# Reordered head of an attention and mixture-of-experts kernel: two router buffers, first-half tiles among the last own ones, two attention tiles ahead of expert 0, tiles spread evenly over the experts

## What is computed

```python
xn = _layernorm(x, axis=-1)
# attention: k = exp(10i * (xn @ Wk)), v = xn @ Wv, 16 heads of 64
out_pos   = real(cumsum(v * rotors) * conj(rotors)) / sqrt(t + 1)
out_assoc = real(cumsum(v * conj(roll(k, 1))) * k) / sqrt(t + 1)
attn = (0.5 * out_pos + 0.5 * out_assoc) @ Wo
# experts: every token goes to one of 8 experts, the argmax of its router logits
p = softmax(xn @ gate_w); e = argmax(p)
ffn = p[e] * (gelu(xn @ w1[e]) @ w2[e])      # 1024 -> 4096 -> 1024
x = x + attn + ffn
```

## Time and profile before

| | |
|---|---|
| median of 3 runs | 1130.99 us (1130.82 to 1131.71) |
| the profiled execution | 1131.58 us; its slowest core, core 1, spans 1129.5 us from the first instruction to the last |
| spans of the eight cores | 1120.4 to 1129.5 us |
| first matmul of expert 0 / 3 / 6 / 7 on core 1 | 131.9 / 474.5 / 819.1 / 926.4 us |
| busy share: TensorE, VectorE, ScalarE, GpSimd | 83%, 61%, 53%, 14% |

### The profile page before, as it was taken

How to read it: one execution, slowest core, us unless ns; L and a number is a source line. 1 busy time by engine, 2 the same in 40 slices (tenths; PEclk the granted TensorE clock), 3 DMA queues, 4 the chain that set the end, 5 groups by cost and what they waited for, 6 DMA issues and landing times.

```text
span 1129.5 us, 18153 instructions; the slowest of 8 cores (1120.4 to 1129.5 us)
## 1 busy us (share of the span) xinstructions
PE 935.5 (83%) x6296; PEld 609.3 (54%) x6296; DVE 692.5 (61%) x1498; ACT 597.7 (53%) x1014; POOL 161.6 (14%) x184
## 2 busy tenths in 40 slices
PE   3756599899899999989878988898889874598683
PEld 2223466566566676566555656565656552354352
DVE  5726535665445334779966998899989992132151
ACT  4354488769965884577437634863486332121000
POOL 0000121001112111121112101210121110221111
PEclk9876599999999999999899998998999986899887
DMA  8999889998999999999999999999999999999983
GB/s 211 228 199 201 182 144 182 168 185 144 165 160 158 180 180 160 157 170 173 160 172 166 172 158 182 167 166 157 170 173 170 157 159 199 199 238 226 213 221 93
DMA packets 123774, 199.64 MB, mean 177 GB/s; under 512 B 4757, under 2 KB 70693, under 8 KB 123680
## 3 DMA queue, kind: packets, MB, share of 16 engines
q0 software_dynamic: 107056, 151.64, 90.5%
q1 hardware_dynamic: 16624, 46.80, 13.1%
...
## 4 chain that ended last, share of the span: by engine, by line
PE 43%; DMA 30%; DVE 11%; issue 7%; ACT 6%; POOL 1%; DVEq 0%; SPq 0%; ACTq 0%; POOLq 0%
DMA ring<-w 13%; PE yb L944 13%; PE wb L627 13%; PE wb L889 10%; DMA yg<-ys,gidx 9%; DMA wos<-wo 4%; PE yb L412 3%; DVE pp L736 3%; DMA ys<-xsr 1%; PE wb L588 1%; DVE pp L741 1%; DVE st L346 1%; DVE pp L743 1%; DVE pp L760 1%; DVE pp L756 1%
## 5 line engine op out<-in xcount | busy, mean ns | idle before, releaser
L889 PE MATMUL wb<-xsT,ring 128*128 128x288 bf16 x2048 | 279.2, 295 | 44.2 <-DMA ring<-w 29.8
L944 PE MATMUL yb<-hT,ring 128*128 128x288 bf16 x2048 | 278.9, 291 | 23.1 <-ACT yT L959 16.2
L889 PEld LDWEIGHTS wb<-xsT,ring 128*128 128x128 bf16 x2048 | 204.2, 101 | 115.4 <-issue 50.8
L944 PEld LDWEIGHTS yb<-hT,ring 128*128 128x128 bf16 x2048 | 202.1, 100 | 92.9 <-issue 32.1
L321 POOL DMA_DIRECT2D ring<-w x128 | 106.0, 832 | 750.7 <-PE yb L944 358.5
L899 ACT ACTIVATE hT<-wb,cfs 128x288 bf16<-128x288 f32 x256 | 118.8, 500 | 131.7 <-PE wb L889 128.6
L674 DVE COPY cs<-bnd 128x2 f32<-128x2 f32 x64 | 10.8, 169 | 168.1 <-ACT cs L658 160.0
L627 PE MATMUL wb<-xT,wks 128*128 128x512 bf16 x384 | 95.9, 395 | 5.3 <-ACT hT L899 5.3
L795 PE MATMUL wb<-wos,z 128*128 128x512 bf16 x256 | 68.0, 414 | 32.6 <-DVE resf L804 18.3
L627 PE MATMUL wb<-xT,wvs 128*128 128x512 bf16 x384 | 92.3, 384 | 0.0
L656 ACT ACTIVATE cs<-cs 128x512 f32<-128x512 f32 x64 | 40.3, 630 | 79.3 <-DVE cs L650 79.2
...
## 6 DMA issues: line engine op xcount, KB each, us to landing
ring<-w POOLq DMA_DIRECT2D x128, 1024.0 KB, 26.0
...
```

The lines of the kernel that those rows point to most:

```text
L889: fn = lambda e, kt=kt, b=b, a=a, k=k: e.matmul(b[:, 0:CAP], ring[k][:, (kt % 4) * DM + a * P:(kt % 4) * DM + (a + 1) * P], xsT[:, kt * CA ...
L944: fn = lambda e, d=d, kc=kc, k=k: e.matmul(yb[d][:, 0:CAP], ring[k][:, (kc % 8) * CH + d * P:(kc % 8) * CH + (d + 1) * P], hT[:, kc * CAP: ...
```

## The change

It has six parts:

- `xn32` becomes two buffers, the second laid over ring buffers 4 and 5; groups of four tiles take them in turn. The copy of a group's logits off PSUM (`take_logits`) is split from `logits` and appended one tile later. Pieces 4 and 5 of the ring wait for the last logits.
- First-half tiles 0 to 3 are loaded, normed and turned within the iterations of own tiles 11 to 15.
- Wk and Wv are loaded at tiles 4 and 7, the ring pieces 0 to 3 at tiles 1, 9, 11 and 13 (before: 1, 4, 7 and 9).
- `route` works on tiles 0 to 7 (appended in iteration 11) and 8 to 15 (behind the loop). `rotor` moves from tiles 4 and 8 to tiles 3 and 7, `rotor_sines` from tile 12 to behind the second `route`, ahead of `take_lists`.
- Units 0 and 1 come before expert 0.
- The lists: experts 0 to 6 held units 0-11, 12-23, 24-33, 34-40, 41-48, 49-56 and 57-64. Now they hold 2-11, 12-21, 22-31, 32-39, 40-47, 48-55 and 56-64. Own tiles of the next chunk (`OS`) stand behind the units in experts 3 to 5; before, one unit came behind them.

```diff
-    x_order = [(xown, i) for i in range(NLT)] + [(xfh, i) for i in range(NLT)]
+    x_order = [(xown, i) for i in range(12)]
+    for i in range(4):
+        x_order += [(xfh, i), (xown, 12 + i)]
+    x_order += [(xfh, i) for i in range(4, NLT)]
...
-                d, ap(b, 0, [[CH, P], [P, 4], [1, P]]), AF.Identity), t_tr, xn32_free[0])
+                d, ap(b, 0, [[CH, P], [P, 4], [1, P]]), AF.Identity), t_tr, xn32_free[g])
...
+    wkv = lambda t_, w_: G.dma(d_wkv, lambda e: e.dma_start(w3(t_), wsrc(w_)), loaded[-1][1])
     for i in range(NLT):
         k, t = st_t[i]
+        f = i - 11
         t_nf = norm(k, xnf[i % 2], t, *nf_free[i % 2])
         pull()
+        if 0 <= f < 4:
+            fh_begin(f)
         begin(i + 1)
         got = turn_own(i, t_nf)
         t_b = rows_own(i, t_nf)
         nf_free[i % 2] = (t_b, got[1][2])
+        if 0 <= f < 4:
+            fh_end(f)
         end(i + 1)
-        if turning:
-            turn_logits(*turning)
-            turning = None
+        if taken:
+            turn_logits(*taken)
+            taken = None
+        if summed:
+            taken = take_logits(*summed)
+            summed = None
         if i - 1 in groups and i < NLT - 1:
-            turning = group(i - 1)
+            summed = group(i - 1)
         evs[i] = put_own(i, got)
-        if i in (1, 4, 7, 9):
+        if f > 0:
+            turn_rows(f - 1)
+        if i in (1, 9, 11, 13):
             feed(loaded[-1][1])
+        if i == 4:
+            wkv(wks, wk)
+        if i == 7:
+            t_wkv[0] = wkv(wvs, wv)
+        if i in (3, 7):
+            rotor(i // 4 * 4, 4)
         if i == 11:
-            G.dma(d_wkv, lambda e: e.dma_start(w3(wks), wsrc(wk)), loaded[-1][1])
-        if i in (4, 8):
-            rotor(i - 4, 4)
-        if i == 12:
-            rotor_sines()
-    route(0, 12)
...
+            route(0, 8)
+    group(14)
+    late = group(NLT - 1)[3]
+    for i in range(8):
         lines_up(i, t_pos[i])
-    t_wkv[0] = G.dma(d_wkv, lambda e: e.dma_start(w3(wvs), wsrc(wv)))
-    fh_norm(0, 1)
-    route(12, 4)
-    for i in range(12, NLT):
+    turn_logits(*take_logits(12, 4, slice(0, CH), late))
+    route(8, 8)
+    rotor_sines()
+    t_u0 = kv(0)
+    for i in range(8, NLT):
         t_m = lines_up(i, t_pos[i])
     take_lists(t_m)
     load_xs(0)
...
     first = {
-        0: mix(US(0, 4), [L(4), L(5, 6, 7), L(6), L(7, 8, 9)]),
-        1: US(12, 16) + [L(12), U(16), L(13, 14, 15), U(17)],
-        2: mix(US(24, 28), OS(0)),
-        3: US(34, 38),
-        4: US(41, 45),
-        5: US(49, 53),
-        6: US(57, 61),
+        0: mix(US(2, 6), [L(4), L(5, 6, 7), L(6), L(7, 8, 9)]),
+        1: US(12, 16) + [L(12), U(16), L(13, 14, 15)],
+        2: US(22, 24) + mix(US(24, 28), OS(0)),
+        3: US(32, 36),
+        4: US(40, 44),
+        5: US(48, 52),
+        6: US(56, 60),
         7: W(0, 8),
     }
...
-        3: US(38, 40) + OS(1) + US(40, 41),
-        4: US(45, 48) + OS(2) + US(48, 49),
-        5: US(53, 56) + OS(3) + US(56, 57),
-        6: US(61, 64) + [load_wo, U(64), load_x4],
+        3: US(36, 40) + OS(1),
+        4: US(44, 48) + OS(2),
+        5: US(52, 56) + OS(3),
+        6: US(60, 64) + [load_wo, U(64), load_x4],
         7: W(8, 16),
```

58 lines of the change are left out of this document (27 added, 31 removed).

## The result

After takes 1164.77 us (median) beside 1131.35 us for the kernel before on the same chip: 1.0292 times as long, 95% interval 1.0274 to 1.031. (One of the four runs of after, with two cores above 1200 us at a lower clock, is left out of the ratio.) The direction of the forecast and its mechanism for experts 3 to 5 were right. Its size was not: I forecast +15 us, measured are +33, and 1164.8 lies above the range's upper end of 1159.

What follows compares the result with a forecast made beforehand. TensorE sets experts 0 to 2; DMA and VectorE stand close from expert 3. Terms 8.3 - 6.9 - 9.9 + 3 + 8.5 + 2.2 + 7.7 + 8 - 5.6 = +15.3 on 1131.6, less 0.6: 1146 us, range 1131 to 1159.

Steps and rivals of the forecast that it cites:

- The coupling in experts 3 to 5: Stage 2's kc 32: TensorE waits 10 us or more for the `yb` copy, one `rneg` later; experts of about 121 us.
- Rival (a): From expert 3 on the DMA keeps the pace, experts 3 to 6 keep 451.9 us: 1125 us, faster; chance 0.13.
- and 1.5 for the ring, which is late there: Expert 3: 1.5 us for the late ring on top of 119.4, making 121 against 112.5, +8.5.
- Expert 2: Six units instead of four in stage 1, ScalarE at least 57.3 us there, less 6.9 in stage 2: +3 (0 to +5).
- Experts 0 and 1: Two tiles fewer in expert 0, -6.9; one tile fewer in each stage of expert 1, -9.9.
- The head: Everything ahead of expert 0: logits and gather late, expert 0 starts at 140 instead of 131.9, +8.3.
- The sines: Head, ahead of `take_lists`: 7.5 us for which VectorE waits before making the lists, half of it beside the marks.
- a sign of being right (about 127): Head: the gather of expert 0's rows issued at about 127 us, 8.3 us late.
- Rival (b): Head: rotors and sines hidden, expert 0 at 129, the rest as forecast: 1135 us; chance 0.14.
- Expert 6: Nine long bodies instead of eight, transposes at kc 37 wait until 99.8 us into the expert: +8.
- Expert 7: Wo one ring piece later, but Wo and queued pieces land sooner as the DMA is no longer behind: -5.6.
- Rival (c): Expert 7: Wo's seven us show in full, with none of the gathers' gain: 1159 us; chance 0.10.

Runs made afterwards that it cites:

- a1: After's kernel with the fourth stage 2 unit of experts 3 to 5 moved from kc 28 to kc 40, reading one tile of the next chunk: 1.006 of before.
- a5: After's kernel with that unit at kc 40 in experts 3 to 5 and the four own tiles later, behind it: 1.018 of before.
- c0: After's kernel unchanged, measured once more on the chip of the runs beside it: 1.0285 of before.
- a4: After's kernel without the loads of four ring pieces in experts 1 and 2, old buffer content used instead: 1.0185 of before.
- c1: After's kernel with four units and two own tiles in stage 1 of expert 2, six units and two own tiles in stage 2: 1.0307 of before.
- a2: After's new head, units 0 and 1 ahead of expert 0, with the lists of the kernel before from there on: 1.0024 of before.
- a3: The head of the kernel before with the new lists from unit 2 on, expert 0 holding units 0 to 11: 1.030 of before.
- b1: After's kernel with the rotors moved from tiles 3 and 7 to behind the norms of tiles 4 and 8: 1.0297 of before.
- b2: After's kernel with the sines' four VectorE instructions moved behind the making of the lists and the gather's issue: 1.0301 of before.
- b4: After's kernel with the load of Wo one ring piece earlier in GpSimd's queue, at kc 37 of expert 6: 1.0258 of before.

## Why the prediction was right in its way and wrong in its size

1. **The coupling in experts 3 to 5: right.** The wait at kc 32 was forecast at 10 us or more, and is 12.8 to 13.9; the start of the first body, the distance of the bodies, the `rneg`, the copy and the gap of 14 us are each within 1 us. Experts 4 and 5 took 122.4 and 121.9 us, forecast 121.0. a1 takes the unit back and the wait falls to 2 to 4 us, with 26 us of the whole (1.0292 to 1.006 of before); with the own tiles where they have to be (a5) it falls as far, with 13 us of the whole. So the wait's 13 us are not its price: without it experts 3 to 5 are 8 to 10 us shorter in a1 and 6 to 7 in a5. Rival (a), the DMA setting the pace, was wrong for these experts: after has next to no ring waits in experts 4 to 6, and only where the coupling is taken away do they return (in experts 4 and 5 of a1, in expert 4 of a5). It is what stands right behind the coupling. In experts 4 and 5 the DMA share is still the fullest row (1.01 and 1.02), and TensorE waits 13 us for an order that no share shows. The Trainium skill (Perfetto Trace Analysis, Identifying the Most-Contended Engine) takes the engine with the highest occupancy as the one to work on, and for the DMA the HBM utilization in place of occupancy. Read as I had read it, that the fullest row sets the time, these experts would have kept theirs, and the trace disagrees: they grew by 3.6 and 8.6 us on the slowest cores, with a wait of 12.96 us in expert 5.

2. **Expert 3: the step that failed is "and 1.5 for the ring, which is late there".** Measured are 8.9 us on core 7 (8.7 as the mean, 8.1 in c0), in series with the coupling, since the longest of these waits lies ahead of the first unit and pushes VectorE's whole chain back. Without them (a4) the expert takes 119.7, against my 119.4 before the ring's term. The numbers for a better term stood in the profile of before. Its expert 3 already had 9.1 us of ring waits, which filled time that TensorE otherwise had to spare:

```profile
PE wb L889 <- DMA ring<-w: 5.3, 2, 3.0
...
PE yb L944 <- DMA ring<-w: 3.8, 1, 3.8
```

I took them to shrink with slower experts. But what counts at expert 3's start is how fast experts 0 to 2 were. Before, these took 342.6 us for 48 pieces, 7.14 each, just over the 7.06 that the DMA needs in experts 3 to 6. My own forecast made them 122.3 - 6.9 + 116.3 - 9.9 + 104 + 3 = 328.8 us, 6.85 a piece, 10 us less than the DMA needs for 48. I never made this division, though I had used 7.06 for the experts behind. Measured are 335.0. The ring had little to lend: its pieces 4 and 5 are issued only at 134.27 us, so it isn't full when expert 0 starts at 140.6, and by the landings in core 7's trace 17, 33 and 49 pieces are there at the starts of experts 1, 2 and 3, one more than has been used each time. In experts 1 and 2 the DMA thus brought 32 pieces in 223.1 us, 6.97 each, where my forecast had 106.4 + 107 = 213.4 us, 6.67 each.

One more thing on expert 3. The prediction and the text ahead of it say that seven units stood ahead of the copy of `yb` before; that is so in experts 4 and 5. Expert 3 held units 34 to 40, with unit 40 behind the copy, so six stood ahead, and the change put two more there. The sum for expert 3 starts from the new order and isn't touched by it.

3. **Expert 2: the same mis-sized term.** Forecast +3, measured +9.2. ScalarE's 56.4 us of stage 1 were right (57.3), but TensorE's waits for the ring, which this term put at nothing, came on top (4.6 us in the mean). Without them a4 has 108.6, +4.5, within the bounds of 0 to +5. With the load on ScalarE taken away instead (c1) nothing is gained. Most of what expert 1 gave came back here: with the lists of before (a2) experts 1 and 2 take 115.8 + 104.3 = 220.1 us, with the new ones (c0) 107.0 + 111.5 = 218.5, so of 8.8 us saved in expert 1 7.2 are back in expert 2. By a4, 2.9 of these 7.2 are the ring and the other 4.3 the fuller stage 1, which the forecast had.

4. **Experts 0 and 1: right together by luck** (-16.8), with two errors that cancel: -10.4 against -6.9 and -6.4 against -9.9. Two runs say something of each. With the old head (a3) expert 1 is 9.6 us shorter than before, the -9.9 of the sum, and behind the new head it gives less (7.5 us in after, 8.7 in c0). With the old lists (a2) expert 0 gives 8.2 us, and the new order of its list 2 more: TensorE's wait for the copy of `yb` in expert 0 is 3.1 us before and in a2, and 0.9 in after. Why a2 gives 8.2 us and not 6.9 stays open.

5. **The head: right in size (+8.7 against +8.3), partly by luck.** As means over the cores the second group's logits start 8.2 us late (forecast 8) and the third's 13.0 (14). But moving the rotors back (b1) gives only 2.3 to 3.7 us at the head's end, since x's loads take over at tiles 12 to 15, which I had not seen. The last logits end 8.2 us late, forecast 5. The sines, which I charged with half of 7.5 us, cost nothing measurable (b2), since the marks wait for unit 0's products anyway, which I had not charged at all. The gather is issued 12.1 us late instead of 8.3, outside what I had named as a sign of being right (about 127). Against that its last part lands 4.3 us after its issue instead of 6.8 (means), and that gives back 2.5 us that I had not forecast. Unit 1's products, which I took as 3.45 us, ran from 132.17 to 137.47, beside the gather as I had it. Rival (b) was wrong: the rotors were not hidden, as I had argued, but the sines, by which I had argued too, were no reason.

6. **Expert 6: right**, +7.0 against +8. The transposes that wait for `cs`'s copy out go on 99.9 us into the expert, forecast 99.8:

```profile
948.71 0.63 PE L926 MATMUL wb<-cbs,yT 128*96 128x128 bf16 x4 [3.03 <-ACT cs L651]
```

7. **Expert 7: right**, -3.0 on the slowest cores and -7.2 in the mean, against -5.6, and for the reason given: a ring that is less behind. In the mean the waits for Wo and for ring pieces fell by 14.1 us together, and nearly half of that (6.2 us) came back as waits of TensorE for VectorE. Rival (c) was wrong; Wo's wait shrank. That its place in the queue would still be worth 5.4 us there (b4) I had left out, for I treated place and lag as one term.

Two readings of the earlier trace rows in the prediction are off, without effect on the sum: TensorE's time to spare is 11 to 16 us an expert from expert 3 on (11.4 in expert 5), not 14 to 16, and its busy share in experts 3 to 6 is 86 to 90%, not 82 to 90.

Neither the range nor the weights of the rivals allowed for two waits that add, one from my sum and one from (a). I had set (a) and the forecast against each other as if only one could hold; in expert 3 both did.
